# A closed-form entmax threshold and a moved set of weight sums in a four-layer fp32 kernel

## The reference, cut to what matters

```python
def entmax_bisect(X, alpha=1.5, n_iter=25):
    inv_am1 = 1.0 / (alpha - 1.0)                      # 2
    Xs = X * (alpha - 1.0)                             # X / 2
    tau_lo = max(Xs) - 1.0
    tau_hi = max(Xs) - (1.0 / d) ** (alpha - 1.0)
    f_lo = sum(maximum(Xs - tau_lo, 0) ** 2) - 1
    dm = tau_hi - tau_lo
    repeat 25 times:
        dm = dm * 0.5
        tau_m = tau_lo + dm
        f_m = sum(maximum(Xs - tau_m, 0) ** 2) - 1
        tau_lo = where(f_m * f_lo >= 0, tau_m, tau_lo)
    p = maximum(Xs - tau_m, 0) ** 2
    return p / sum(p)
# layer 1: 8 tiles of 512 tokens, C = 256 channels, E = 8 experts, F = 1024
gates  = entmax(x @ Wr + br); gates = where(gates > 1e-9, gates, 0)
out    = sum over e of gates[:, e] * (relu(x @ W1[e] + b1[e]) @ W2[e] + b2[e])
```

## Time and profile before

| | before |
|---|---|
| median of 2 runs | 4234.84 us |
| profiled execution | 4233.45 us |
| its span, first to last instruction | 4231.6 us |
| PE busy | 4069.9 us (96%) |
| DVE busy | 2698.8 us (64%) |
| ACT busy | 1886.0 us (45%) |
| GpSimd busy | 343.8 us (8%) |
| mean granted TensorE clock | 0.985 |

### The profile page before, as it was taken

How to read it: one execution, slowest core, us unless ns; L and a number is a source line. 1 busy time by engine, 2 the same in 40 slices (tenths; PEclk the granted TensorE clock), 3 DMA queues, 4 the chain that set the end, 5 groups by cost and what they waited for, 6 DMA issues and landing times. The chain is left out here.

```text
span 4231.6 us, 60173 instructions
## 1 busy us (share of the span) xinstructions
PE 4069.9 (96%) x21117; PEld 2730.8 (65%) x21117; DVE 2698.8 (64%) x6277; ACT 1886.0 (45%) x3774; POOL 343.8 (8%) x456
## 2 busy tenths in 40 slices
PE   6999988999999999999999999999998998999999
PEld 3545446878878788887878887666665554333333
DVE  6666657565564746647465564586787987666765
ACT  2444444434354443534435354355544221555555
POOL 0222211101010020111101010000000000000000
PEclk9999998999999999999999999999999999999999
DMA  3111102212122121222212121100000001011110
GB/s 90 17 17 17 36 7 85 87 61 89 69 86 82 60 87 66 96 71 76 77 61 102 60 91 57 47 1 1 1 1 22 1 1 25 17 24 21 26 24 22
DMA packets 61907, 198.67 MB, mean 47 GB/s; under 512 B 11256, under 2 KB 21120, under 8 KB 52744
## 3 DMA queue, kind: packets, MB, share of 16 engines
q1 hardware_dynamic: 60784, 194.55, 14.9%
q10 hardware_dynamic: 816, 0.20, 0.0%
HBM read 171.11 MB, written 4.46 MB: 41 GB/s over the span
## 5 line engine op out<-in xcount | busy, mean ns | idle before, releaser
L1211 PE MATMUL l_exp_out<-l_w,l_hidden 128*128 128x256 f32 x4096 | 914.4, 381 | 0.6
L1211 PEld LDWEIGHTS l_exp_out<-l_w,l_hidden 128*128 128x128 f32 x4096 | 768.8, 190 | 117.2 <-issue 9.1
L1369 ACT ACTIVATE l_hidden<-l_hid 128x512 f32<-128x512 f32 x384 | 227.7, 596 | 619.2 <-PE l_hid L1171 618.2
L1735 DVE SCALAR_TENSOR_TENSOR l_moe<-l_exp_out,l_gates,l_moe 128x256 f32<-128x256 f32 x256 | 123.8, 484 | 502.8 <-PE l_exp_out L1211 498.3
L507 DVE TENSOR_REDUCE l3f_row_max<-l3f_bank 128x1 f32<-128x512 f32 x512 | 327.9, 686 | 177.1 <-PE l3f_bank L387 176.7
L1645 DVE TENSOR_TENSOR l_hidden<-l_hid,l_hidden 128x512 f32<-128x512 f32 x384 | 262.1, 690 | 239.4 <-PE l_hid L1171 233.5
L463 ACT ACTIVATE l3f_prob_t<-l3f_bank 128x512 f32<-128x512 f32 x512 | 277.2, 596 | 206.3 <-PE l3f_bank L394 206.3
L1171 PE MATMUL l_hid<-l_x_sums,l_w_sums 128*128 128x256 f32 x1536 | 346.9, 382 | 13.2 <-DVE l_hidden L1645 13.2
L1171 PEld LDWEIGHTS l_hid<-l_x_sums,l_w_sums 128*128 128x128 f32 x1536 | 292.6, 191 | 56.1 <-issue 16.4
L504 DVE CUSTOM_DVE_ANT_0 l_masked<-l_bank,l_mask 128x256 f32<-128x256 f32 (+3 forms) x512 | 226.7, 487 | 157.3 <-PE l_bank L387 156.4
L1381 ACT ACTIVATE l_hidden<-l_hidden,l_w 128x256 f32<-128x256 f32 (+1 forms) x512 | 279.0, 605 | 84.1 <-DVE l_hidden L1645 83.8
(11 more groups left out here) (516 smaller groups left out, 6916.7 us busy)
## 6 DMA issues: line engine op xcount, KB each, us to landing
l_w<-in_w SPq DMA_DIRECT2D x64, 1024.0 KB, 4.8
l_w_first<-in_w SPq DMA_DIRECT2D x64, 512.0 KB
l_w_second<-in_w SPq DMA_DIRECT2D x64, 512.0 KB, 3.8
l_mix<-l_cum SPq DMA_DIRECT2D x32, 512.0 KB, 4.6
l_qk_t<-l_packed SPq DMA_DIRECT2D x128, 64.0 KB
l3f_qk_t<-l3f_packed SPq DMA_DIRECT2D x128, 64.0 KB
all_x<-in_x SPq DMA_DIRECT2D x8, 512.0 KB, 6.1
out_x<-all_x SPq DMA_DIRECT2D x7, 512.0 KB, 3.0
```

Source lines behind the costliest of these rows:

```text
L1211: ins = nc.tensor.matmul(bank[:, 0:C], hidden[:, e % 2, f, j * P:(j + 1) * P], w2[:, e % 2, f, :], start=f == 0, stop=f == HF - 1)
L1369: hid.empty(nc.scalar.activation(hidden_block(e, half_f, x, half_t), pair(bank), ACT.Copy), (e, x, which, turn))
L1735: exp_out.empty(V.scalar_tensor_tensor(moe[:, j, :], bank[:, 0:C], gates[:, j, e:e + 1], moe[:, j, :], ALU.mult, ALU.add), (e, j))
```

## The change

1. The bisection goes. `route_sums` makes for each of the 8 values of a token three sums over the values not below it (count, sum, sum of squares), by three multiplications or comparisons and three reductions over 256 columns, and from them the quantity under the root. ACT takes the root (`root`). `route_end` picks the threshold, makes one Newton step of it and normalises. For tiles 1 to 7 `route_sums` stands on DVE behind expert 6's second expert sum, and `root` on ACT behind the root for the norm. For tile 0 `root` stands on ACT behind the four z activations, ahead of the first xb copy.
2. `begin` is now `route_end`, then `gate_all`, then the adds of experts 0 and 1 with nothing among them.
3. All 64 sets of W1 sums are on GpSimd. S1 waits for product b1 of the expert before, S3 for a2, S4 for b2.
4. Five tiles of the bisection are gone, `count`, `mean` and `spread` come in.

The core of the diff:

```diff
+                def root(t):
+                    act.wait_ge(spread_ready, t + 1)
+                    nc.scalar.activation(spread[:, :, :], spread[:, :, :], ACT.Sqrt).then_inc(root_ready, 1)
...
-                if b:
+                if not b:
+                    root(0)
+                else:
                     exp_out.wait_emptied_through(act, b - 1, [(E - 1, j) for j in range(TJ)])
...
                         nc.scalar.activation(rms[:, :], rms[:, :], ACT.Sqrt).then_inc(rms_ready, 1)
+                        if not is_last:
+                            root(b + 1)
...
             input_sums(0)
-            weight_sums(0, None)
-            weight_sums(1, 0)
-            weight_sums(2, 1)
-            pool.wait_ge(d_ready, 1)
+            weight_sums(0)
             for b in range(B):
-                is_last = b == B - 1
+                n = b * E
+                weight_sums(n + 1)
+                weight_sums(n + 2)
+                weight_sums(n + 3)
+                if b == 0:
+                    pool.wait_ge(d_ready, 1)
                 mask(b, 0)
                 skip(b)
                 mask(b, 1)
                 scale_c(b, 1)
+                weight_sums(n + 4)
                 mask(b, 2)
                 sum_squares(b, 0)
+                weight_sums(n + 5)
                 mask(b, 3)
                 scale_c(b, 2)
                 sum_squares(b, 1)
+                weight_sums(n + 6)
                 scale_c(b, 3)
                 sum_squares(b, 2)
+                weight_sums(n + 7)
                 sum_squares(b, 3)
-                if not is_last:
+                if b < B - 1:
+                    weight_sums(n + 8)
                     input_sums(b + 1)
...
+                st.link(V.tensor_tensor(half[:, :, :], half[:, :, :], tau[:, :].unsqueeze(2).to_broadcast(experts), ALU.subtract))
+                st.link(V.tensor_scalar(half[:, :, :], half[:, :, :], -2.0, None, ALU.max))
+                bound, value = half[:, :, :].unsqueeze(3).to_broadcast(pairs), half[:, :, :].unsqueeze(2).to_broadcast(pairs)
+                st.link(V.tensor_tensor(at_least, value, bound, ALU.is_ge))
+                V.tensor_reduce(count[:, :, :], at_least, AX, ALU.add)
+                st.link(V.tensor_tensor(weighed, at_least, value, ALU.mult))
+                V.tensor_reduce(mean[:, :, :], weighed, AX, ALU.add)
+                st.link(V.tensor_tensor(at_least, weighed, value, ALU.mult))
+                st.link(V.tensor_reduce(spread[:, :, :], at_least, AX, ALU.add))
+                st.link(V.reciprocal(count[:, :, :], count[:, :, :]))
...
+                V.tensor_scalar(spread[:, :, :], spread[:, :, :], -1.0, 0.0, ALU.mult, ALU.max).then_inc(spread_ready, 1)
...
+            def route_end(st, it):
+                dve.wait_ge(root_ready, it + 1)
+                st.link(V.tensor_tensor(mean[:, :, :], mean[:, :, :], spread[:, :, :], ALU.subtract))
+                st.link(V.tensor_tensor(over[:, :, :], mean[:, :, :], half[:, :, :], ALU.is_gt))
+                st.link(V.scalar_tensor_tensor(mean[:, :, :], over[:, :, :], -4.0, mean[:, :, :], ALU.mult, ALU.add))
+                st.link(V.tensor_reduce(tau[:, :], mean[:, :, :], AX, ALU.max))
+                route_mass(st)
+                st.link(V.tensor_reduce(step[:, :], spread[:, :, :], AX, ALU.add))
+                st.link(V.reciprocal(step[:, :], step[:, :]))
+                st.link(V.scalar_tensor_tensor(step[:, :], mass[:, :], -1.0, step[:, :], ALU.add, ALU.mult))
+                st.link(V.scalar_tensor_tensor(tau[:, :], step[:, :], 0.5, tau[:, :], ALU.mult, ALU.add))
+                route_mass(st)
                 st.link(V.reciprocal(step[:, :], mass[:, :]))
...
-            def begin(st, it, turns, gate=None):
...
+            def begin(st, it, gate=None):
+                route_end(st, it)
+                if gate is not None:
+                    gate()
+                for e in range(2):
+                    add_11(it, e)
+                    add_22(it, e)
...
-                weight_sums(b, 3, (b, 2))
...
-                    if e + 2 < E:
-                        weight_sums(b, e + 2, (b, e + 1))
-                    elif not is_last:
-                        weight_sums(b + 1, 0, (b, E - 1))
...
-                        if e == 6 and not is_last:
-                            if j == 0:
-                                route_start(st, jobs, b)
-                            else:
-                                route(st, [j - 1])
+                        if (e, j) == (6, 1) and not is_last:
+                            route_sums(st, jobs, b)
...
-                    begin(st, b + 1, (8, 2, 1), gate_all)
+                    begin(st, b + 1, gate_all)
```

More of the change, by code:

```diff
@@ L1599, in _ @@
             V.tensor_copy(wbcs[:, :, S_ROW:], ws).then_inc(small_weights, 1)
-            for i in range(BISECT):
-                V.memset(powers[:, i:i + 1], 0.5 ** (i + 1))
             dve.sem_inc(squares_summed, 1)
@@ L1605, in _, with route_sums @@
             experts = [P, TJ, E]
-            def route_start(st, ring, it):
+            pairs = [P, TJ, E, E]
+            at_least, weighed = (squares[:, 2 * i:2 * i + 2, :].rearrange("p f l -> p (f l)").rearrange("p (j i k) -> p j i k", i=E, k=E)
+                                 for i in range(2))
+            def route_sums(st, ring, it):
                 bank = ring.wait_filled(dve, it, "small")
@@ L1621, in route_start, with route_mass @@
+                st.link(V.scalar_tensor_tensor(spread[:, :, :], spread[:, :, :], -1.0, count[:, :, :], ALU.add, ALU.mult))
+                V.tensor_scalar(spread[:, :, :], spread[:, :, :], -1.0, 0.0, ALU.mult, ALU.max).then_inc(spread_ready, 1)
+            def route_mass(st):
+                st.link(V.tensor_tensor(over[:, :, :], half[:, :, :], tau[:, :].unsqueeze(2).to_broadcast(experts), ALU.subtract))
+                V.tensor_scalar(spread[:, :, :], over[:, :, :], 0.0, None, ALU.max)
                 st.link(V.scalar_tensor_tensor(part[:, :, :], over[:, :, :], 0.0, over[:, :, :], ALU.max, ALU.mult))
@@ L1654, in add_12 @@
                 add(it, e, "b", 2, 0, 1, ("a", 1))
-            def weight_sums(it, e, before):
-                n = it * E + e
-                low, high = w1_first[:, 0:HALF_F], w1_first[:, HALF_F:F]
-                second = w1_second[:, e % 2, :]
-                dve.wait_ge(first_loaded, 16 * (n + 1))
-                dve.wait_ge(second_loaded[e % 2], 16 * (it * (E // 2) + e // 2 + 1))
-                hid.wait_filled(dve, before[0], (before[1], 1, "b", 2))
-                V.tensor_tensor(w1_sums[:, S1, :], high, second[:, HALF_F:F], ALU.add).then_inc(w1_summed, 1)
-                V.tensor_tensor(w1_sums[:, S3, :], low, high, ALU.subtract).then_inc(w1_summed, 1)
-                dve.wait_ge(w1_summed, n * 4 + 1)
-                V.tensor_tensor(w1_sums[:, S2, :], w1_sums[:, S1, :], low, ALU.subtract).then_inc(w1_summed, 1)
-                dve.wait_ge(w1_summed, n * 4 + 3)
-                V.tensor_tensor(w1_sums[:, S4, :], second[:, 0:HALF_F], w1_sums[:, S2, :], ALU.subtract).then_inc(w1_summed, 1)
-            def begin(st, it, turns, gate=None):
-                at = iter(range(BISECT - sum(turns), BISECT))
-                steps = [[next(at) for _ in range(n)] for n in turns]
-                adds = [(f, e) for e in range(2) for f in (add_11, add_22, add_12)]
-                route(st, steps[0])
-                for n, (f, e) in enumerate(adds):
-                    f(it, e)
-                    if f is add_12 and gate is not None:
-                        weight_sums(it, e + 1, (it, e))
-                    if (f, e) == (add_12, 0) and gate is not None:
-                        gate()
-                    if n + 1 < len(steps):
-                        route(st, steps[n + 1])
-                    if n + 2 == len(steps):
-                        route_end(st)
-                    if (f, e) == (add_22, 1):
+            def begin(st, it, gate=None):
[5 more added lines that the diff above has]
+                    add_22(it, e)
+                    if e == 1:
                         bank = ring.wait_filled(dve, it, "gt")
                         ring.empty(V.tensor_copy(gates_t, bank[0:E, :]), "gt")
+                    add_12(it, e)
                 for n in range(2):
@@ L1694, in _ @@
             first_steps = Steps(dve, dve_step, 0)
-            route_start(first_steps, first, 0)
-            begin(first_steps, 0, (9, 3, 3, 3, 3, 4))
+            route_sums(first_steps, first, 0)
+            begin(first_steps, 0)
             for f in range(FT):
```

63 lines of the change are left out of this document (24 added, 39 removed).

## The result

The changed kernel takes **4200.91 us** (median of two runs, 4197.91 and 4203.91) against 4234.84: ratio 0.9925, 95% interval 0.9909 to 0.9942. Times 4234.84, the interval of the ratio is 4196 to 4210 us. The profiled execution took 4203.91 us, with a span of 4202.1.

What follows compares the result with a forecast made beforehand. PE was taken as the bound, busy 254.06 of 255 us in tile 1, with waits for DVE mainly in tile 0. Gains of 20.1 + 7.8 = 27.9 us gave 4207 us against the median, range 4202 to 4224.

Steps and rivals of the forecast that it cites:

- Tile 0, gates: Tile 0, expert 0's first product to `expert_out(0)`: without the bisection no add waits for the gates; 20.1 us gained.
- up to 1.0: Tile 0, DVE's steps to the value under the root: one instruction stands behind a GpSimd sum, up to 1.0 us.
- ACT charge of 0.5 us: Tile 0: ACT's table load and root make the second xb copy 0.5 us later, charged to PE; bounds 0 and 5.
- the wait ahead of b1: Product b1 of expert 1: PE's 0.98 us wait, put down to W1 sums and `gate_all`, goes; 8 x 0.98 = 7.8 us.
- the other 14 steps: Rest of each bisection in later tiles: lies where DVE has nothing late, so removing it was priced at nothing.
- The later tiles' sum: Tiles 1 to 6: the gain forecast was the 0.98 us wait ahead of b1 in each tile.
- still faster: Rival: short waits of `expert_out(0)` go too, 7 x 0.6 = 4 us more, 4203 us; chance 0.07.
- The last tile: Tile 7: a 0.9 us wait goes; the 7.4 us wait from the variances of seven tiles on DVE stays.
- The sums on GpSimd cost nothing: 61 moved W1 sets: GpSimd goes to about 67 us in a 255 us window, sums in time, DVE unblocked; cost 0.
- The rival on the other side: GpSimd's sums block one DVE instruction per moved set, 1.03 us each, 63 us: 4270 us; slower than before: chance 0.06.

Runs made afterwards that it cites:

- the closed form alone: Changed kernel with the W1 sums of 61 of the 64 sets back on DVE, the bisection still gone: 4206.86 us, ratio 0.9948.
- the doubled sums: Changed kernel with every W1 sum on GpSimd done twice into the same place: ratio 0.9932, tile 0 at 253.02 us.
- the sums alone: Kernel before with all W1 sums moved to GpSimd, bisection and place of the gate product kept: 4250.97 us, ratio 1.0042.
- the loop written out: DVE's loop over tiles written out, in the changed kernel: 4201.24 us, ratio 0.9926; in the kernel before: ratio 0.9990.
- the gate product moved: Kernel with W1 sums on DVE and no bisection, gate product put back behind expert 0's adds and W1 sums: ratio 0.9939.

## Why the prediction was right, and where it was off

In layer 1 the forecast was 27.9 us and 33.2 came: 0.9 us more in tile 0, 3.1 in tiles 1 to 6 and 1.3 in tile 7.

*Tile 0, gates: right.* Forecast 20.1 plus 0.98, measured 21.94, and the closed form alone gives it. Its 256-column steps take 0.42 us, as interpolated; one step was blocked for 0.99 us against "up to 1.0". The **ACT charge of 0.5 us was not there**: from the first z product to expert 0 PE takes 14.46 us now, 14.51 before. ACT in the changed kernel, answering to the earlier trace rows:

```profile
653.97 1.28 ACT L1418 ACT_TABLE_LOAD   x1
655.26 0.23 ACT L1418 ACTIVATE l_spread<-l_spread 128x32 f32<-128x32 f32 x1
...
657.43 0.58 ACT L1364 ACTIVATE l_xbc<-l_bank 128x512 f32<-128x512 f32 x1
```

The root was not late. Counted from the first z product, the routing begins at 2.45 us (2.49 before) and the root at 9.70, where the forecast has it at 9.8. (DVE has 19 instructions up to the value under the root and not 17; they take 6.4 us, forecast 6.0.) The second xb copy comes at 11.87 us in place of 11.60, so 0.27 us later and not 0.5, and PE did not wait for it. With the doubled sums the root waited 1.58 us for DVE, and PE waited 0.85.

On the Trainium skill, "ScalarE: Activation LUTs", section "What ACT_TABLE_LOAD costs", with its further 1.38 us of drain on each switch: this trace, too, does not show it. The root starts 1.29 us after the start of its load of 1.28 us (655.26 and 653.97), and PE lost nothing.

*Tiles 1 to 7, the wait ahead of b1: the size right, the cause incomplete, and so in part luck.* The 0.98 us went, in seven tiles. The step that failed is "It waits for `add_11(1)` ... because the W1 sums and then `gate_all` ... stand ahead of it". These two alone make no wait. The bisection in `begin`, by the rows its last step, was the third part. The prediction priced "the other 14 steps" at nothing and did not name the 11 in `begin` at all. The size came out right because the change removed all three parts at once; with the sums alone moved, the same reading forecast a gain and the kernel lost 2.01 us a tile.

*The later tiles' sum was too small:* 1.49 us a tile in place of 0.98. In the mean of six tiles, 1.32 us came up to `expert_out(0)` and 0.17 in it. In tile 1, beside the 0.98, a0 of expert 1 had stood 0.17 us late, and twice 0.07 us went around it. `expert_out(0)` takes 14.29 us in place of 14.46: 0.08 as the bias copies are no longer behind W1 sums (they end 0.80 us behind its start in place of 0.88), the rest because the idle time ahead of the taps happened to be shorter (3.06 in place of 3.15 us in the mean). That is the rival "still faster" in part, with 0.17 us a tile in place of its 0.6. It was argued away because "those lie in the conv taps, which do not change". The tap's own row showed otherwise, had it been read: the 3.2 us of idle time ahead of it are the loop's turn, 0.66 us a tile in the kernel before. Only the loop written out took that away.

*The last tile:* 2.29 us. The stretch to `expert_out(0)` gives 1.31; another 1.00 is the 16 products behind the 7.4 us wait, 5.58 us in place of 6.58, at another granted clock. The loop written out had 6.68 there and the same wait, so that 1.0 us is not the change's.

*The sums on GpSimd cost nothing: right for this kernel.* GpSimd's busy time in the tile window is 65.97 us, forecast 67. The sums take 1.27 us, the adds 0.69, and PE waits for neither. But "cost: 0" holds only because the closed form came with them. Alone they cost 13.4 us in layer 1.

*The rival on the other side* had the right mechanism in the wrong place. It named the mix product between adds; what was blocked, in the kernel without the closed form, were three small steps of the bisection, and they cost 2.0 us a tile net, 1.2 where the clock did not fall.

*The range* missed the median by 1.1 us at the low end, since its low end was the case "still faster" without any spread. The early part of the program alone spreads over 6 us. So the miss by 1.1 us says little; what was too small in the sum is the 5.3 us above.

## What to carry to other kernels

Two edits in one change need the two kernels with one edit each: here one half is worth 26 us, the other costs 13 alone, and together they are worth 33. A wait behind a queue of small pieces has no single cause: add up all that stands between the last instruction in time and the late one, and see by how much PE is late. When work goes to GpSimd, look at which DVE instructions with inputs in SBUF lie in the stretch where it will run, however narrow they are.

Read also the idle time "<-issue": a loop's turn on an engine can sit on the path of another.

## What the runs showed of the hardware

- The turn of DVE's loop (206 busy instructions in the tile window of the changed kernel, 408 before) leaves it idle for 2.95 to 3.27 us in most kernels, and for 4.07 to 4.32 us in the closed form alone, with and without the gate product moved (4.12 there). What makes it longer there stays open.
- DVE instructions of 128x4 were held off by GpSimd's sums (0.73 and 0.90 us in place of 0.15 and 0.16) like one of 128x32 (1.22 in place of 0.19). With the doubled sums a TENSOR_SCALAR with one input was held off too (1.18 us in place of 0.18 at 645.67, 2.98 in place of 1.14 for four of 128x256), while reductions were not (0.18 us at 1195.89 in the sums alone).
- That is what the Trainium skill, "SBUF — State Buffer", section "Who interferes with whom", says of `tensor_scalar` in its two-port modes and of `tensor_reduce`; by that rule, these traces agree.
- A wait of PE of one length can end at either clock: behind 2.49 us the granted clock was 0.63 in one tile and 1.00 in the next, and eight products took 3.44 and 1.97 us. Behind the 7.4 us wait 16 products took 5.58, 6.58 and 6.68 us in three kernels.
- The thirteen kernels do the same up to layer 1, and the time at which they reach it differs by up to 6 us. Effects of a few us are read from cuts inside the profile, not from the median.
